# A recurrence beside a mixture-of-experts layer on one core: the first block in pairs and groups, the output sums of the experts phase moved to TensorE, and the expert weights sent earlier

## The reference

```python
xn = layernorm(x)
# attention branch (gated delta rule), state S is 16 x 16 for each of 16 x 16 (sequence, head)
h  = layernorm(xn) * ln1_g + ln1_b
q, k, v = h @ Wq * 16**-0.5, normalised(h @ Wk), h @ Wv
beta, g = sigmoid(h @ Wb), sigmoid(h @ Wg)
for t in range(512):
    S = S * g[t]
    S = S + beta[t] * outer(k[t], v[t] - k[t] @ S)
    o[t] = q[t] @ S
a = xn + o @ Wo + bo
attn = a + gelu(layernorm(a) * ln2_g + ln2_b @ w1 + b1) @ w2 + b2      # the two-layer net after it
# experts branch
w, e = top8(softmax(xn @ router_w.T))
ffn = sum_k w_k * expert_{e_k}(xn) + shared(xn)       # silu(x @ Wg_e) * (x @ Wu_e) @ Wd_e, at most 128 tokens each
out = x + attn + ffn
```

## Time and profile before

| | |
|---|---|
| median of 3 runs (lowest to highest) | 1865.07 us (1864.67 to 1867.93) |
| the profiled execution's own time / its span | 1868.96 us / 1866.9 us |
| busy of the span: DVE, POOL, PE, ACT | 91%, 85%, 76%, 43% |
| first step of the recurrence | 72.06 us |
| experts phase with the iteration after it, I = 19 to 35 | 594.24 to 1092.08 us |

### The profile page before, as it was taken

One profiled execution on the slowest core, in us unless ns is written; L12 is line 12 of the kernel. 1 busy time (PEld: TensorE's weight loads), 2 busy tenths in 40 slices (PEclk: granted clock), 3 DMA queues, 4 the chain that ended last, 5 costly groups with the idle time before them and its releaser, 6 DMA issues. The chain is left out here.

```text
span 1866.9 us, 31499 instructions
## 1 busy us (share of the span) xinstructions
PE 1422.3 (76%) x8846; PEld 1231.1 (66%) x8846; DVE 1693.1 (91%) x4988; ACT 810.6 (43%) x2548; POOL 1591.9 (85%) x1354
## 2 busy tenths in 40 slices
PE   6776777877863677575666559898998999889858
PEld 5665666766753576464655548777776877768647
DVE  3699999999999999899977989998999999899980
ACT  4534454545444544345432235444543453334313
POOL 5379999899998889888897789999999999999961
PEclk9978878878875887777877669998999999989889
DMA  8674234533346657846667422242223311211110
GB/s 182 167 167 122 70 100 118 142 83 98 93 117 166 158 135 177 214 107 172 147 155 212 102 52 61 68 127 83 72 56 106 90 57 49 66 50 56 46 46 22
DMA packets 337169, 201.24 MB, mean 108 GB/s; under 512 B 208226, under 2 KB 327716, under 8 KB 336996
## 3 DMA queue, kind: packets, MB, share of 16 engines
q1 hardware_dynamic: 318724, 168.43, 34.7%
q0 software_dynamic: 15616, 30.55, 7.3%
q10 hardware_dynamic: 2656, 0.26, 0.1%
HBM read 127.58 MB, written 71.60 MB: 107 GB/s over the span
## 5 line engine op out<-in xcount | busy, mean ns | idle before, releaser
L846 POOL TENSOR_TENSOR rp<-S,qs 128x2048 f32<-128x2048 f32 x113 | 521.2, 4612 | 43.1 <-DVE S L1169 29.6
L1169 DVE SCALAR_TENSOR_TENSOR S<-S,gwin,bank 128x256 f32<-128x256 f32 x1024 | 496.6, 485 | 0.3
L1159 DVE TENSOR_REDUCE nu<-vwin 128x16 f32<-128x272 f32 x1024 | 451.5, 441 | 0.3
L1163 DVE TENSOR_TENSOR bank<-nu,bank 128x256 f32<-128x256 f32 x1024 | 443.5, 433 | 0.6
L1154 DVE TENSOR_TENSOR vwin<-S,bank 128x256 f32<-128x256 f32 x1024 | 434.8, 425 | 0.0
L854 POOL TENSOR_TENSOR r<-rp 128x1024 f32<-128x1024 f32 x113 | 273.6, 2421 | 7.0
L1510 ACT ACTIVATE region<-bank,b_s 128x128 f32<-128x128 f32 x512 | 144.8, 364 | 274.1 <-PE bank L1821 274.1
L1821 PEld LDWEIGHTS bank<-region 128*128 128x128 f32 x2048 | 247.6, 200 | 21.5 <-issue 16.2
L1821 PE MATMUL bank<-region 128*128 128x128 f32 x2048 | 260.0, 287 | 2.2 <-ACT region L1500 2.2
L1701 PE MATMUL bank<-xaT,wqkvg 128*128 128x128 f32 (+1 forms) x1792 | 240.5, 287 | 23.1 <-ACT xaT L1355 19.9
L1701 PEld LDWEIGHTS bank<-xaT,wqkvg 128*128 128x128 f32 (+1 forms) x1792 | 215.0, 189 | 37.3 <-ACT xaT L1355 23.9
(11 more groups left out here) (170 smaller groups left out, 2285.4 us busy)
## 6 DMA issues: line engine op xcount, KB each, us to landing
qkv_d<-stg SPq DMA_DIRECT2D x192, 128.0 KB, 3.1
region<-in_L_ffn_w_gate SPq DMA_DIRECT2D x64, 192.0 KB, 3.9
region<-in_L_ffn_w_up SPq DMA_DIRECT2D x64, 192.0 KB, 4.1
region<-in_L_ffn_w_down SPq DMA_DIRECT2D x64, 192.0 KB, 4.9
region<-in_L_attn_x SPq DMA_DIRECT2D x16, 512.0 KB, 7.3
region<-in_L_attn_x SPq DMA_DIRECT2D x32, 256.0 KB, 4.4
xw_d<-region SPq DMA_DIRECT2D x32, 256.0 KB, 4.0
acc_d<-region SPq DMA_DIRECT2D x32, 256.0 KB, 4.0
```

Of the source, the lines that this page charges most:

```text
L846: g.tensor_tensor(rp[:, :, :].rearrange("p (a v) d -> p a v d", v=DH), S[h][:, lo:lo + HS].rearrange("p t s (v d) -> p (t s) v d", v=DH), ...
L1159: m[G] = mark(v.tensor_reduce(nu[:, G], products_of(I, s, G)[1], AX.X, ALU.add))
L1163: m[G] = mark(v.tensor_tensor(outer[G].rearrange("p (v d) -> p v d", v=DH), nu[:, G].unsqueeze(2).to_broadcast([P, DH, DH]), key(L, s, G), ...
L1169: ins = v.scalar_tensor_tensor(S[h][:, s, G], earlier(h, s, G), gwin[:, I // NB2 & 1, G, 1, t:t + 1], outer[G], ALU.mult, ALU.subtract)
```

## The change

**First block.** The 16 front tiles of blocks 0 and 1 start earlier: block 0's x comes in four pairs of tiles (`first_pair`), each with its own statistics on DVE (`pair_statistics`) and factors on POOL (`pair_factors`); Wq, Wb and Wg are loaded from ACT's queue, Wk and Wv between the pairs; PE runs 16 identity products on constants first. The gates' weights stand interleaved (`wgate`), so a tile's gates go to DRAM, and come back, in one transfer (`gat_d` is laid out anew, for every block). A store is four transfers, k and gates first. The second half's keys are loaded in two groups, tiles 4 to 6 and tile 7. The factors are made for tokens 0 to 7 only before the first step (`head` on DVE, `first_head` on ACT); those of tokens 8 to 63 by ACT and POOL during iteration 0 (`stage_squares`, `square_sums`, `norm_gates`, `key_scales`, `scale_values`, DVE's part at steps 4 and 7).

**Experts phase.** Where `on_tensor(I)` holds (13 iterations: 19 to 33 without 23 and 31), both halves are only multiplied on POOL (`rp`, `rx`). PE adds them in the next iteration: 16 products with the identity accumulate into the free quarter `rsum` of bank LG, for each half (`read_rows`), and ACT copies the 128 sums to `oblk` (`rows_out`). DVE's `read_sum` is gone. In iteration 34 POOL adds both halves.

**Weights.** `experts` of the next iteration is issued in two parts, two experts ahead of `next_window` and `front_store`, two behind.

```diff
-def summed(I):
-    return X0 <= I < X1 and I % NB2 != NB2 - 1
+def on_tensor(I):
+    return X0 <= I < X1 - 1 and I % NB2 != NB2 - 1
...
+        rsum = LG[:, 3 * P:4 * P]
...  (SP)
-                if X0 <= I < X1:
-                    experts(I - X0)
+                if I == X0:
+                    experts(0, range(RT))
...
+                if X0 <= I < X1 - 1:
+                    experts(I - X0 + 1, (0, 1))
                 if I >= R1 and j < 2 and I // NB2 + 1 < NBLK:
                     next_window(I // NB2, j)
                 if I >= R1 and f is not None:
                     front_store(f, f // NB2, f % NB2, h)
+                if X0 <= I < X1 - 1:
+                    experts(I - X0 + 1, (2, 3))
...  (POOL, reads and products)
+                pool.wait_ge(row_sums[0], tensor_sums_before(I))
                 g.tensor_tensor(
                     rp[:, :, :].rearrange("p (a v) d -> p a v d", v=DH),
...
+                if half == 0 and on_tensor(I):
+                    return
...
-                pool.wait_ge(x_sums, 2 * sums_before(I))
+                pool.wait_ge(row_sums[1], tensor_sums_before(I))
...  (DVE)
-                    if s >= 6 and summed(I - 1):
-                        read_sum(I - 1, s - 6)
...
+                    if I == 0 and s == 4:
+                        key_factors(0)
+                    if I == 0 and s == ST - 1:
+                        dve.wait_ge(vals_ready, 1)
+                        stage_factors(0, ST, BLK)
...  (ACT)
+            def rows_out(I, half):
+                act.wait_ge(row_sums[half], tensor_sums_before(I) + 1)
+                act.wait_ge(o_stored, (I >> 3) * OST)
+                t0 = I % NB2 * ST + half * HS
+                a_.activation(oblk[:, :, :, t0:t0 + HS], rsum.rearrange("p (t s v) -> p s v t", s=2, v=DH), ACT.Copy).then_inc(row_out[half], 1)
...
+                if f == NB2 + 1:
+                    first_head()
+                    stage_squares(0, 0)
                 if f == NB2 + 2:
-                    key_norms(0)
+                    stage_squares(0, 1)
                     stage(0, 0)
+                if f == NB2 + 3:
+                    key_norms(0)
...  (PE)
+            for n in range(16):
+                mm(R1B[:, 0:P], ident[:, :], ones[:, :], start=True, stop=True)
...
+            def read_rows(I, half):
+
+                pe.wait_ge(prod_done, I * 2 + (3 + half))
+                pe.wait_ge(slot_used, min(I + 1 - R1, NR))
+                for n in range(2):
+                    pe.wait_ge(row_out[n], tensor_sums_before(I) + (half if n == 0 else 0))
+                src = (rp, rx)[half]
+                for d in range(DH):
+                    last = mm(rsum, ident[:, :], src[:, :, d], start=(d == 0), stop=(d == DH - 1))
+                last.then_inc(row_sums[half], 1)
```

More of the change, by code:

```diff
@@ L159, with tensor_sums_before @@
 ROUNDS_END = R1 + NR - 1
-def summed(I):
-    return X0 <= I < X1 and I % NB2 != NB2 - 1
-def sums_before(I):
-    return sum(summed(i) for i in range(I))
+def on_tensor(I):
+    return X0 <= I < X1 - 1 and I % NB2 != NB2 - 1
+def tensor_sums_before(I):
+    return sum(on_tensor(i) for i in range(I))
 NYW = 6
 LATE = 3
-FST = 5 * 16
-WLD = 4 * 16
+FST = 4 * 16
+WLD = 3 * 16
 KLD = 16
@@ L581, in weights_store, with experts @@
                     sp.dma_start(wt_r[k, q, b], xwt[h][BLK * b:BLK * (b + 1), :, :]).then_inc(w_stored[h], 16)
-            def experts(n):
-                for r in range(RT):
+            def experts(n, turns):
+                for r in turns:
                     e = n * RT + r
@@ L891, in scatter @@
                                      yw[e % NYW], None, compute_op=ALU.add).then_inc(sc_done, 16)
[L893 removed]
             for s in range(2):
[L895 removed]
+                square_sums(0, s)
+            norm_gates(0)
+            key_scales(0)
+            for s in range(2):
                 scale_values(0, s)
+            relink()
             def residual(I):
@@ L1338, in _ @@
                 a_.dma_start(lncol[:, m, :], w.rearrange("(c p) -> p c", p=P), allow_slow_non_contiguous=True).then_inc(ln_ld, 16)
+            weights_load(act, 0)
+            for m, w in enumerate((Wb, Wg)):
+                a_.dma_start(wgate_in[:, :, m], w.rearrange("(c p) n -> p c n", p=P)).then_inc(raw_ld[3], 16)
             def front_norm(f, i, first=False, behind=0):
-                if first:
+                if first and f < NB2:
+                    act.wait_ge(pair_done, f // 2 + 1)
+                elif first:
                     act.wait_ge(stats_done, f // NB2 + 1)
@@ L1700, in front_columns @@
                 for c in range(DC):
-                    last = mm(dst[0:n, :], wqkvg[:, c, i * P:i * P + n], xaT[h][:, c, :], start=(c == 0), stop=(c == DC - 1))
+                    w = wqkvg[:, c, i * P:i * P + n] if i < 6 else wgate[:, c].rearrange("p h w -> p (h w)")
+                    last = mm(dst[0:n, :], w, xaT[h][:, c, :], start=(c == 0), stop=(c == DC - 1))
                 return last
@@ L1898, in expert_iteration @@
                 expert_T(n, q + 2, 2, hx)
+                if on_tensor(I - 1):
+                    read_rows(I - 1, 0)
                 front_qk(f, h)
                 if t < NR:
+                    pe.wait_ge(row_out[0], tensor_sums_before(I))
                     slot_round(t)
@@ L1907, in expert_iteration @@
                 expert_gu(n, q + 3, 3)
+                if on_tensor(I - 1):
+                    if t < NR:
+                        pe.wait_ge(slot_mm, t + 1)
+                    read_rows(I - 1, 1)
                 expert_y(n * RT + 2, 2)
```

247 lines of the change are left out of this document (152 added, 95 removed).

## The result

The changed kernel takes **1953.45 us** (median of 4 runs, 1951.76 to 1955.4) against 1866.05 us for the kernel before beside it (1864.67 to 1867.93): a ratio of 1.0463, 95% interval 1.0444 to 1.0481. It is slower by 4.6%; forecast were 1824 us, and 1893 us was the end of the range.

The account below looks back on a forecast made before the run. The prediction took POOL to bound the experts phase (461 us, -36.8 us); with -5 us from the first block that made about -42 us, from the median 1824 us (-2.3%), range 1797 to 1893 us.

Parts of the forecast that it names:

- The record's price: PE's strided sums in the experts phase: 0.12 us a record taken as likeliest, 0.20 to 0.23 us as the upper price.
- PE's room in an iteration: Experts phase: PE at 25.1 us an iteration with the sums, 430 us in all, stays beneath POOL's 461 us.
- Without both it is 17.4 us: PE's work in iteration 28, 21.2 us, less the slower clock of the first gate and up and a 2.0 us wait.
- With PE at 25 of 27 us there is room: Experts phase: PE can take work queued behind a late `read_rows`, its own work being 25 of an iteration's 27 us.
- the first rival: Strided stream costs memory time, PE bounds the experts phase at 32.0 us an iteration: 1880 to 1897 us; chance 0.33.
- Between: Rival: records at 0.15 to 0.18 us, or PE, POOL and DVE waiting in a ring: 1829 to 1853 us; chance 0.12.
- The queues behind `read_rows`: Experts phase: a late `read_rows` holds up PE's `front_qk` and down products, then ACT's `expert_out` and POOL's scatters; no cost.
- POOL's bound of 461 us: Experts phase falls from 497.8 to 461 us: POOL loses a tree, first two scatters 4.56 us apart, 39 us saved.
- DVE's reductions and waits: Experts phase: DVE loses reductions (34.0 us), may lose waits (29.9 + 5.1 us): 429 us if no other engine holds it.
- The first block, -5 us: Start: first step at about 57 instead of 72 us, most given back in iteration 1; -5 us, bounds -2 and -10.
- Weights ahead "at nothing": Experts' weights issued ahead of the store: 12 issues of 0.5 us on SP move, costed at nothing.
- ACT's two copies, the shared bank, the hand-overs: Experts phase: ACT's copies (0.3 to 0.45 us each) hidden; bank LG puts `read_rows(., 0)` some 6 us into DVE's iteration.

Follow-up runs that it names:

- e3: Changed kernel with POOL writing the products so that PE streams 128 neighbouring columns in each of the 16 products: 1877.68 us, ratio 1.0034.
- e6: Changed kernel with both streams moved to the end of PE's iteration, behind the down products, columns still 64 bytes apart: 1867.69 us, ratio 1.0027.
- e5: Changed kernel with contiguous columns and both streams moved to the end of PE's iteration, behind the down products: 1834.62 us, ratio 0.9840.
- e12: e5 with the x loads of tiles 16 to 31 issued by SP, as in the kernel before: 1831.98 us, ratio 0.9825.
- e2: Changed kernel with 1 instead of 16 products for each half's sums on PE, all waits and hand-overs kept: 1837.88 us, ratio 0.9822.
- e8: Kernel before with only the experts' weights sent ahead of the next window's loads and the front's store: 1857.28 us, ratio 0.9970.
- e4: Changed kernel with the experts phase's sums as before (POOL's tree, DVE's reductions), first block and weights' order as changed: 1861.61 us, ratio 0.9953.
- e7: Kernel before with only the first block (and the gates' tensor in one piece) as changed: 1862.97 us, ratio 0.9995.
- e10: e4 with the x loads of tiles 16 to 31 issued by SP, as in the kernel before, instead of POOL: 1850.94 us, ratio 0.9922.

## Why the prediction was wrong

Two of its steps failed. The ratios to the kernel before, with each mended alone and both together:

| | columns strided | columns side by side |
|---|---|---|
| streams where the change has them | 1.0463 (changed) | 1.0034 (e3) |
| streams in PE's gap | 1.0027 (e6) | 0.9840 (e5) |

Either mend alone takes off 4.3% (80 us), and the other then only 1.9% (35 us) more: once the ring is near the pace of POOL and DVE, a microsecond out of it is no longer worth a microsecond. So the price of one error depends on which is mended first. To 0.9825 (e12, x loads) it is another 0.15% or 3 us, which is within the intervals, and 0.45%, 8 us, are left to the forecast's 0.978.

- **The record's price: wrong.** The step "If the extra is counted in the array's own cycles ... it is 0.8 ns at 2.4 GHz and vanishes in the 0.94" was an argument about cycles set against two rows of a measured time. The changed kernel shows 0.223 us a record, where the rival had 0.20 to 0.23, and e3 shows that the layout is the cause. Nor is it a count of the array's cycles: a strided record takes 0.218 us at either clock level (e6). The Trainium skill's rule that was cited (Advanced Engine Details and Errata, SBUF Cachelines) agrees at all four distances tried, 4, 8, 16 and 64 bytes.
- **PE's room in an iteration: wrong, in the forecast and in every rival.** "Without both it is 17.4 us" took PE's waits out, and "With PE at 25 of 27 us there is room" took the gap behind the last down product for slack. It is ACT's tail, in series with PE's work, and it stays as long as before however much PE has to do. Even cheap records give 17.4 + 7.7 + 6.8 = 31.9 us and not 25.1 (e3: 30.5 to 34.2 in iterations 26 to 31), and dear ones 38.5 to 40.3 and not 32, which is why the result lies beyond the first rival's 1897 us. The trace of before had it: 7.2 and 5.9 us between iterations at the two turns shown, and ACT busy in just that stretch. (The rival "Between" does name a ring, but of PE, POOL and DVE, at 28 us an iteration; ACT is not in it.)
- **The queues behind `read_rows`:** named rightly, down products, `expert_out`, scatters. What was missing is that ACT's tail is queued behind the last of them.
- **POOL's bound of 461 us: met in number, partly by luck.** Where PE no longer holds the phase it takes 460.6 us (e5) and 462.0 (e2). But the first two scatters are 5.22 us (e5) and 5.51 us (e2) apart in the mean, not 4.56, so 27 to 31 us are saved and not 39. The order of the weights, costed at nothing, takes 11 us off the phase by itself (e8), which makes up for it.
- **DVE's reductions and waits:** they are gone, as counted, and their place is taken by 125 us of waits at the products that need silu (100.3 us for silu, 25.1 with no releaser shown).
- **The first block, -5 us: wrong, for a term it left out.** Tile 0 started at 15.0 us (14.0 forecast). The keys came not 8 us earlier but 1.8 us later (61.3 against 59.5), and iteration 2 began 2.5 to 3.5 us late (e4, e7, changed), not 5 early. The x loads' move to POOL's queue had been given no cost; with it undone (e10) iteration 2 begins 4.5 us early, near the forecast.
- **Weights ahead "at nothing": too low.** They give 0.3%.
- **ACT's two copies, the shared bank, the hand-overs:** rightly small (e2).
- **The sum** has a small slip: 1865.07 - 41.8 is 1823 us and -2.2%, where it says 1824 and -2.3%.

## To carry to other kernels

Before an engine's gap is counted as room, ask what the other engines do in it: a gap that recurs with the iteration, with a lightly loaded engine busy through it and a hand-over at both ends, is a link of a ring, and work added to the engine anywhere else is added to the period. Put the new work into the gap itself, or move the other engine's tail out of it. And arrange an operand so that the side that is on the path reads it packed: here POOL's strided write cost 0.03 us, PE's strided read 3.4 us a half.

## What the runs showed of the hardware

- A float32 stream of 128 columns through PE took 0.117 us a record with columns 4 bytes apart, 0.119 with 8, 0.233 with 16 and 0.223 with 64: a step, not a slope.
- The packed stream's records come every 0.111 us at the 2.4 GHz level and every 0.213 us at 1.2 GHz (e5). The strided stream's come every 0.218 us at both (e6): strided, PE is as slow at full clock as at half.
- POOL's 2048-element product took 4.51 or 5.10 us with a packed write and 4.54 or 5.13 with elements 512 bytes apart, where ACT's strided write of 1024 elements had cost 0.9 us more.
- With two MB of loads issued on POOL's queue just ahead of the first stores, ACT waited 5.8 us for a 128 KB store to land (5.74 in e4); with the same loads on SP's queue (e10), 2.3 us.
